# Four lanes in place of two in the last two node stages of a four-layer graph network

## The chip, the cores and the metric

The kernel runs on one core of one Trainium2 chip. The metric is the time on the device in microseconds, from one launch of the whole program. Three runs of the kernel before were timed.

## The reference

Four graph layers run one after the other on 6250 nodes of 128 features and 206250 directed edges. After each layer the input is added to its output and the sum is normalized over the features (mean 0, variance 1). Layer 0 sums edge features per target node and sends the sum and the node through a two-layer network. Layer 1 is edge attention with two norms and a feed-forward part. The two layers that matter here end in node work:

```
# layer 2: edges through a network, summed per target, then a network per node
agg  = segment_sum(relu(e_in @ We1 + be1) @ We2 + be2, dst)
x    = layernorm(x + (x + relu([x, agg] @ Wn1 + bn1) @ Wn2 + bn2))
# layer 3: sum over edges weighted by the degrees of both ends
deg  = segment_sum(1, row);  norm = deg[row]**-0.5 * deg[col]**-0.5
x    = layernorm(x + segment_sum(norm * x[col], row) @ W.T + b)
```

## The kernel before, in words

Node features stand transposed in SBUF: `x` and `acc` are [128 features, 6656 columns], the columns padded from 6250 nodes. They are cut into 26 tiles of T = 256 columns (TJ = 2 halves of 128). The program is a row of blocks, one after the other, each with a queue written out by hand for every engine: prepare, edge sums, layer0_nodes, layer1_edges, layer1_nodes, layer2_edges, **layer2_nodes** (line 1819), layer3_edges, **layer3_nodes** (line 2132). Only the two in bold are changed. Each starts when the block ahead of it has ended on all engines.

A node stage runs 13 steps (STEPS) of two tiles, the lanes (LANES = 2). In a step each engine goes through its phases in a fixed order, and in each phase over the lanes. An engine waits for a semaphore ahead of a piece of work, so lane 1 can fill the time in which lane 0 travels to another engine and back, but no engine starts the next step before its last phase of this one. The loops are hardware loops; offsets into `x`, `acc` and `counts` come from a register. `bank(l, b)` gives each lane four PSUM banks of its own, of which a tile of 256 fp32 columns fills half of one.

The phases of TensorE in layer2_nodes are, in order: **A**, L1834 (`We2` by `acc`) and L1836 (`be2` by the edge counts, which stand on 2 rows); **B**, L1839 and L1842 (the two halves of `Wn1`, the second after ScalarE has copied A's result, L1863); **C**, L1846 (`Wn2`, after ScalarE's ReLU, L1866); then the norm of `norm_pe`: **D**, L723 (subtract the mean, after VectorE's sum, L1900); **E**, L728 (variances, after ScalarE's squares, L741; results of one column); **F**, L734 (spread the inverse deviations, after ScalarE's root, L745, and VectorE's reciprocal, L750); and **G**, L1852 (two transposes, after VectorE's product L756). VectorE then scales the transposed rows (L1908), GpSimd splits them into three bf16 parts (four operations, L765 to L774), and SyncE stores them to DRAM (L1933), where layer3_edges reads them. Every matmul here is fp32 and appears as two passes.

In layer3_nodes TensorE's phases are: spreading four columns of degree factors over the partitions (L2143, four matmuls a tile), after VectorE's two small copies (L2167, L2168); L2149 (`W3`), after VectorE has done three dependent operations per tile (L2173, L2176, L2179); and D, E and F as above, after VectorE's L2184. VectorE's L756 ends a tile, and SyncE stores it to the output (L2197). GpSimd has no part in it.

What guards the reuse of a lane: TensorE's phase A waits until the rows of the same lane's tile of the step before have been scaled (`y_scaled`); VectorE's L1908 waits until GpSimd has split that tile (`split_step`); GpSimd waits for that tile's store (`y_stored`); VectorE's L756 in layer 3 waits for the output store (`out_stored`).

Of the kernel before, what the change touches and what calls it, by code (L numbers as in the profile page):

```python
# [5 lines left out]
P = 128  # L6
D = 128
# [7 lines left out]
T = 256  # L15
TJ = T // P
# [26 lines left out]
def gnn_program(nc, xT, edge_attr, src_index, src_id, dst_id, dst_rows, consts,  # L43
# [18 lines left out]
    with ctx:  # L62
# [647 lines left out]
        out_stored = [sem(f"out_stored{l}") for l in range(LANES)]  # L710

        def node_tiles(scope, layer):

            tiles = {name: [sb(f"{name}{layer}_{l}", [P, T], scope=scope) for l in range(LANES)]
                     for name in ("tmp", "res", "cen", "sqr", "y", "y2")}
            tiles["std"] = [sb(f"std{layer}_{l}", [P, TJ], scope=scope) for l in range(LANES)]
            tiles["inv"] = [sb(f"inv{layer}_{l}", [P, TJ], scope=scope) for l in range(LANES)]
            return tiles

        def norm_pe(pe, t, nth, ready, count_of):  # L720
            for l in range(LANES):
                pe.wait_ge(ready, count_of(l) + 1)
                nc.tensor.matmul(bank(l, 1)[:, 0:T], centre_m, t["res"][l][:, :], start=True, stop=True  # L723
                                 ).then_inc(centred_ps, 1)
            for l in range(LANES):
# [5 lines left out]
            for l in range(LANES):  # L731
# [6 lines left out]
        def norm_act(act, t, nth):  # L738
            for l in range(LANES):
# [3 lines left out]
            for l in range(LANES):  # L743
# [3 lines left out]
        def norm_dve(dve, t, nth, y_free=None):  # L747
            for l in range(LANES):
                dve.wait_ge(std_ready, nth + l + 1)
                dve.reciprocal(t["inv"][l][:, :], t["std"][l][:, :]).then_inc(inverse_ready, 1)  # L750
            for l in range(LANES):
# [1055 lines left out]
        y_stored = [sem(f"y_stored{l}") for l in range(LANES)]  # L1807
        nth2 = 4 * NTILES
        with ExitStack() as scope:
            t = node_tiles(scope, 2)  # L1810
            relu2_sb = [sb(f"relu2_{l}", [P, T], scope=scope) for l in range(LANES)]
            node_rows = [sb(f"y_f{l}", [P, TJ, D], scope=scope) for l in range(LANES)]
            y_parts = [sb(f"y_parts{l}", [P, TJ, 3, D], BF16, scope=scope) for l in range(LANES)]
            rest = [sb(f"y_rest{l}", [P, TJ, D], scope=scope) for l in range(LANES)]
# [4 lines left out]
            with nc.Block("layer2_nodes") as block:  # L1819
                @block.tensor  # L1820
                def _(pe):
# [6 lines left out]
                    with loop(pe, 0, STEPS) as n:  # L1828
                        def tile(l):
                            return n * LANES + l  # L1830

                        for l in range(LANES):
                            pe.wait_ge(y_scaled, tile(l) * TJ + TJ)
                            nc.tensor.matmul(bank(l, 0)[:, 0:T], we2_sb[:, :], acc[:, columns(tile(l))],  # L1834
                                             start=True, stop=False)
                            nc.tensor.matmul(bank(l, 0)[:, 0:T], be2_rows[:, :], counts[:, columns(tile(l))],  # L1836
                                             start=False, stop=True).then_inc(agg_ps2, 1)
                        for l in range(LANES):
                            nc.tensor.matmul(bank(l, 2)[:, 0:T], wn1_sb[:, 0, :], x[:, columns(tile(l))],  # L1839
                                             start=True, stop=False)  # L1840
                            pe.wait_ge(agg2, tile(l) + 1)
                            nc.tensor.matmul(bank(l, 2)[:, 0:T], wn1_sb[:, 1, :], t["tmp"][l][:, :],  # L1842
                                             start=False, stop=True).then_inc(hidden_ps2, 1)
                        for l in range(LANES):
                            pe.wait_ge(hidden2, tile(l) + 1)
                            nc.tensor.matmul(bank(l, 0)[:, 0:T], wn2_sb[:, :], relu2_sb[l][:, :],  # L1846
                                             start=True, stop=True).then_inc(mlp2, 1)
                        norm_pe(pe, t, nth2 + n * LANES, sum2, tile)
                        for l in range(LANES):
                            pe.wait_ge(normed, nth2 + tile(l) + 1)  # L1850
                            for j in range(TJ):
                                nc.tensor.transpose(bank(l, 2 * j)[:, 0:P], t["y"][l][:, j * P:(j + 1) * P],  # L1852
                                                    ident).then_inc(y_ps, 1)

                @block.scalar
                def _(act):
                    act.wait_ge(degree, 3)
                    act.activation(dis[:, :], deg_raw[:, :], ACT.Sqrt).then_inc(degree_sqrt, 1)
                    with loop(act, 0, STEPS) as n:
                        load_sqrt_table(act)  # L1860
                        for l in range(LANES):
                            act.wait_ge(agg_ps2, n * LANES + l + 1)
                            act.activation(t["tmp"][l][:, :], bank(l, 0)[:, 0:T], ACT.Copy).then_inc(agg2, 1)  # L1863
                        for l in range(LANES):
                            act.wait_ge(hidden_ps2, n * LANES + l + 1)
                            act.activation(relu2_sb[l][:, :], bank(l, 2)[:, 0:T], ACT.Relu,  # L1866
                                           bias=v("bn1")).then_inc(hidden2, 1)
                        norm_act(act, t, nth2 + n * LANES)
                        for l in range(LANES):
                            act.wait_ge(normed, nth2 + n * LANES + l + 1)  # L1870
                            act.activation(x[:, columns(n * LANES + l)], t["y"][l][:, :], ACT.Copy).then_inc(x_kept, 1)

                @block.vector
                def _(dve):
# [17 lines left out]
                    with loop(dve, 0, STEPS) as n:  # L1892
                        for l in range(LANES):
                            c = n * LANES + l
                            dve.tensor_scalar(t["y2"][l][:, :], x[:, columns(c)], 2.0, v("bn2"), ALU.mult,
                                              ALU.add).then_inc(twice2, 1)
                        for l in range(LANES):
                            dve.wait_ge(twice2, n * LANES + l + 1)
                            dve.wait_ge(mlp2, n * LANES + l + 1)
                            dve.tensor_tensor(t["res"][l][:, :], bank(l, 0)[:, 0:T], t["y2"][l][:, :],  # L1900
                                              ALU.add).then_inc(sum2, 1)
                        norm_dve(dve, t, nth2 + n * LANES)
# [364 lines left out]
```

## Time and profile before

| | us |
|---|---|
| median of 3 runs (lowest, highest) | 5868.11 (5867.2, 5871.65) |
| the profiled execution's own time | 5868.77 |
| its span, first to last instruction | 5866.9 |
| PE, matmuls: busy | 5316.1 (91%) |
| DVE busy | 4674.9 (80%) |
| ACT busy | 2572.2 (44%) |
| POOL busy | 2071.5 (35%) |
| mean granted TensorE clock | 0.965 of full speed |

The profile is of one execution. PE is TensorE's matmuls and PEld its weight loads, DVE is VectorE, ACT ScalarE, POOL GpSimd, SP SyncE. Times in the trace count from the span's start, and L1834 is line 1834 of the kernel before. In a view of busy time by stretch, PEclk is the clock that TensorE was granted, 1.00 for 2.4 GHz and 0.50 for 1.2 GHz. In the timeline, operations of one kind that follow each other are merged: "x8" means eight of them in that time, and a matmul's end is modelled.

### The profile page before, as it was taken

The numbers are of one execution on the slowest core, as the hardware profiler recorded it, in microseconds if no ns is written. First come the engines' busy times: TensorE is split into PE (matmuls) and PEld (weight loads), VectorE is DVE, ScalarE is ACT, GpSimd is POOL, SyncE is SP. The second block draws the span as 40 slices with busy tenths as digits, with TensorE's granted clock in tenths as the row PEclk, the third lists the DMA queues.
The fourth block names the chain that finished last, engine by engine and source line by source line (L and its number), as shares of the span: only waits on it lengthen the run. The fifth ranks groups of instructions, "written<-read, shape, count | busy, mean of one in ns | idle before, by whom it ended". The sixth has DMA issues, their size and how long they took to land. (4 is left out here: it accounts for less than half of the span.)

```text
span 5866.9 us, 170714 instructions
## 1 busy us (share of the span) xinstructions
PE 5316.1 (91%) x58518; PEld 4689.3 (80%) x58518; DVE 4674.9 (80%) x8022; ACT 2572.2 (44%) x5031; POOL 2071.5 (35%) x1980
## 2 busy tenths in 40 slices
PE   2999989799999999999997779999999997699987
PEld 2888877699999999999995569999999995466645
DVE  6999962588888888888884469999999993488874
ACT  0000024344444344444432347777777762366641
POOL 1444436333333333333332335555555551100000
PEclk9999999999999999999997989999999997899978
DMA  7444421222222222222220123333333330100000
GB/s 114 153 152 152 152 84 68 96 95 92 92 94 90 94 92 92 92 89 97 92 85 17 38 90 130 133 133 131 129 134 131 132 107 17 54 0 1 0 1 24
DMA packets 206213, 523.68 MB, mean 89 GB/s; under 512 B 33555, under 2 KB 85398, under 8 KB 199318
## 3 DMA queue, kind: packets, MB, share of 16 engines
q1 hardware_dynamic: 195936, 518.35, 26.1%
q10 hardware_dynamic: 10179, 4.02, 0.3%
q8 instruction: 62, 1.02, 0.1%
q14 instruction: 36, 0.29, 0.0%
HBM read 485.12 MB, written 37.19 MB: 89 GB/s over the span
## 5 line engine op out<-in xcount | busy, mean ns | idle before, releaser
L1276 PE MATMUL ps<-kv_table,stage 128*128 128x256 bf16 x7644 | 1252.8, 273 | 29.2 <-DVE stage L1132 27.5
L1556 POOL TENSOR_TENSOR parts<-rest 128x512 bf16<-128x512 f32 x624 | 699.4, 1130 | 622.5 <-DVE rest L1609 622.3
L1201 ACT ACTIVATE q_kept<-ps 128x512 f32<-128x512 f32 (+1 forms) x676 | 392.5, 581 | 1157.5 <-PE ps L1279 1157.5
L1746 PE MATMUL ps<-a_table,stage 128*128 128x128 bf16 x7644 | 843.6, 219 | 33.6 <-DVE stage L1585 33.6
L1749 PE MATMUL ps<-window,stage 128*128 128x128 bf16 x7800 | 862.8, 220 | 0.0
L1279 PE MATMUL ps<-window,stage 128*128 128x128 bf16 x7800 | 861.2, 220 | 0.0
L1248 POOL TENSOR_TENSOR message<-message 128x512 f32<-128x512 f32 (+1 forms) x468 | 482.0, 1030 | 986.7 <-ACT message L1210 986.6
L1276 PEld LDWEIGHTS ps<-kv_table,stage 128*128 128x128 bf16 x7644 | 667.6, 98 | 70.7 <-issue 28.1
L1279 PEld LDWEIGHTS ps<-window,stage 128*128 128x128 bf16 x7800 | 654.2, 98 | 59.5
L1140 DVE TENSOR_TENSOR product<-ps,q_kept 128x512 f32<-128x512 f32 (+1 forms) x676 | 451.2, 667 | 300.3 <-ACT message L1203 261.0
L1746 PEld LDWEIGHTS ps<-a_table,stage 128*128 128x128 bf16 x7644 | 534.5, 98 | 34.1 <-issue 34.0
L2075 PE MATMUL ps<-pairs,y_window 128*128 128x512 bf16 (+1 forms) x2028 | 532.2, 371 | 28.0 <-ACT pairs L2043 28.0
L1749 PEld LDWEIGHTS ps<-window,stage 128*128 128x128 bf16 x7800 | 545.7, 98 | 0.0
L1291 PE MATMUL ps<-message,slot_hot 128*128 128x136 f32 x3536 | 515.6, 288 | 32.6 <-POOL message L1248 32.5
L1665 ACT ACTIVATE parts<-ps 128x512 bf16<-128x512 f32 x624 | 370.4, 594 | 332.5 <-PE ps L1749 330.6
L2043 ACT ACTIVATE pairs<-ps 128x512 bf16<-128x512 f32 (+1 forms) x676 | 386.7, 572 | 259.4 <-PE ps L2067 210.4
L1760 PE MATMUL ps<-parts,slot_hot 128*128 128x258 bf16 x2496 | 491.1, 273 | 5.4 <-issue 3.5
L412 POOL TENSOR_TENSOR pay<-bucket_hot,vals 128x1550 bf16<-128x1550 bf16 x104 | 324.7, 3140 | 483.4 <-PE ps L393 370.8
L1291 PEld LDWEIGHTS ps<-message,slot_hot 128*128 128x128 f32 x3536 | 442.2, 190 | 50.6 <-POOL message L1248 32.2
L1762 PE MATMUL ps<-rest,slot_hot 128*128 128x128 bf16 x2600 | 476.8, 222 | 0.0
L1144 DVE TENSOR_REDUCE score<-product 128x32 f32<-128x512 f32 (+1 forms) x676 | 450.1, 666 | 23.2
L1152 DVE TENSOR_TENSOR slot_hot<-iota,slots 128x512 f32<-128x512 f32 (+1 forms) x676 | 454.0, 672 | 0.0
(350 smaller groups left out, 10473.0 us busy)
## 6 DMA issues: line engine op xcount, KB each, us to landing
stage<-lists SPq DMA_DIRECT2D x312, 768.0 KB, 4.1
edges<-in_edge_attr SPq DMA_DIRECT2D x52, 1984.0 KB, 7.7
stage<-lists SPq DMA_DIRECT2D x104, 896.0 KB, 5.4
window<-qkv_rows SPq DMA_DIRECT2D x52, 288.0 KB, 4.7
qkv_rows<-kv_table SPq DMA_DIRECT2D x26, 384.0 KB, 2.5
window<-ab_rows SPq DMA_DIRECT2D x52, 192.0 KB, 4.4
qkv_rows<-q_parts SPq DMA_DIRECT2D x26, 192.0 KB, 2.0
ab_rows<-a_table SPq DMA_DIRECT2D x26, 192.0 KB, 2.0
```

What stands on the lines that cost most here:

```text
L1140: dve.tensor_tensor(product[:, 0:nt, :], kv_ps[n % 2][:, 0:nt, 0:D], q_kept[n % 2][:, 0:nt, :], ALU.mult).then_inc(product1, 1)
L1152: dve.tensor_tensor(slot_hot[n % 2][:, 0:nt, :], over_chunks(iota1[:, :], nt), over_columns(slots[:, ds(g, 1), 0, 4 * b:4 * b + nt] .rearr ...
L1248: pool.tensor_tensor(values, values, message[n % 3][:, 0:nt, D:D + HEADS].unsqueeze(3) .broadcast_to([P, nt, HEADS, HEAD]), ALU.mult).then ...
L1276: nc.tensor.matmul(kv_ps[n % 2][:, i, :], from_src, kv_table[:, tile, q, :], start=(q == 0), stop=(q == 2))
L1279: last = nc.tensor.matmul(q_ps[n % 2][:, i, :], own, window[d][:, q * D:(q + 1) * D], start=(q == 0), stop=(q == 2))
L1291: last = nc.tensor.matmul(ps[:, 6 + d, 0:D + HEADS], slot_hot[n % 2][:, i, :], message[n % 3][:, i, :], start=(tile == 0), stop=(tile == S ...
L1556: pool.tensor_tensor(parts_of(n)[:, 0:nt, D:2 * D], rest[BUFFER[n]][:, 0:nt, :], middle[BUFFER[n]][:, 0:nt, :], ALU.subtract).then_inc(low ...
L1746: nc.tensor.matmul(to[:, i, :], from_src, a_table[:, tile, q, :], start=(q == 0), stop=False)
L1749: last = nc.tensor.matmul(to[:, i, :], own, window[d][:, (3 + q) * D:(4 + q) * D], start=False, stop=(q == 2))
L1760: nc.tensor.matmul(ps[:, 6 + d, 0:DIRECT], slot_hot[BUFFER[n]][:, :, i], parts_of(n)[:, i, :], start=(tile == 0), stop=False)
L1762: last = nc.tensor.matmul(ps[:, 6 + d, DIRECT:SUMS], slot_hot[BUFFER[n]][:, :, i], middle[BUFFER[n]][:, i, :], start=False, stop=(tile == ...
L2075: last = nc.tensor.matmul(ps[:, 4 + quad % 2, 0:nt * P], y_window[:, ds(i * 4 + d, 1), q * D:(q + 1) * D] .rearrange("p s f -> p (s f)"), ...
```

## The change

`WIDE` = 4 lanes are used in the two blocks. The 26 tiles go in six looped steps of four (`WIDE_STEPS`), and after the loop a seventh step of two (`REST_LANES`) is written out with constant offsets. A lane has two PSUM banks in place of four, and `half(l, b)` gives quarter b as half a bank, so that quarters 0 and 1 share one and quarters 2 and 3 the other. The tiles of SBUF that belong to a lane are doubled in number. The waits that guard reuse now look back four tiles. The operations and their number per tile, and their order within a lane, stay as they are; the order between lanes follows the loops. The other node stages keep two lanes and `bank`. The diff, cut:

```diff
+        WIDE = 4
+        WIDE_STEPS = NTILES // WIDE
+        REST_LANES = NTILES - WIDE * WIDE_STEPS
+        out_stored = [sem(f"out_stored{l}") for l in range(WIDE)]
+
+        def half(l, b):
+
+            return ps[:, 2 * l + b // 2, b % 2 * T:b % 2 * T + T]
+
+        def wide_steps(eng, step):
+
+            with loop(eng, 0, WIDE_STEPS) as n:
+                step(n, n * WIDE, WIDE)
+            if REST_LANES:
+                step(WIDE_STEPS, WIDE * WIDE_STEPS, REST_LANES)
...
-        def norm_pe(pe, t, nth, ready, count_of):
-            for l in range(LANES):
+        def norm_pe(pe, t, nth, ready, count_of, lanes=LANES, bank=bank):
+            for l in range(lanes):
...
@@ layer2_nodes, TensorE
-                    with loop(pe, 0, STEPS) as n:
+                    def step(n, first, lanes):
...
-                        for l in range(LANES):
+                        for l in range(lanes):
                             pe.wait_ge(y_scaled, tile(l) * TJ + TJ)
-                            nc.tensor.matmul(bank(l, 0)[:, 0:T], we2_sb[:, :], acc[:, columns(tile(l))],
+                            nc.tensor.matmul(half(l, 0), we2_sb[:, :], acc[:, columns(tile(l))],
                                              start=True, stop=False)
...
-                                nc.tensor.transpose(bank(l, 2 * j)[:, 0:P], t["y"][l][:, j * P:(j + 1) * P],
+                                nc.tensor.transpose(half(l, 2 * j)[:, 0:P], t["y"][l][:, j * P:(j + 1) * P],
                                                     ident).then_inc(y_ps, 1)
+
+                    wide_steps(pe, step)
...
@@ layer2_nodes, VectorE, GpSimd and SyncE
-                                dve.wait_ge(split_step, SPLITS2 + (n * LANES + l) * SPLITS + SPLITS - ROWS_AHEAD // 2)
+                                dve.wait_ge(split_step, SPLITS2 + (first + l) * SPLITS + SPLITS - SPLITS * WIDE)
...
-                            pool.wait_ge(y_scaled, c * TJ + TJ + LANES * TJ)
+                            pool.wait_ge(y_scaled, c * TJ + TJ + WIDE * TJ)
...
-                    sp.sem_inc(y_scaled, LANES * TJ)
-                    for l in range(LANES):
+                    sp.sem_inc(y_scaled, WIDE * TJ)
+                    for l in range(WIDE):
                         sp.sem_inc(y_stored[l], 16)
...
@@ layer3_nodes
-            t = node_tiles(scope, 3)
-            scales = [sb(f"scales{l}", [P, 2 * TJ], scope=scope) for l in range(LANES)]
+            t = node_tiles(scope, 3, WIDE)
+
+            def whole(l):
+
+                return ps[:, 2 * l, :]
+
+            scales = [sb(f"scales{l}", [P, 2 * TJ], scope=scope) for l in range(WIDE)]
...
-                                last = nc.tensor.matmul(bank(l, 0)[:, j * P:(j + 1) * P],
+                                last = nc.tensor.matmul(whole(l)[:, j * P:(j + 1) * P],
                                                         scales[l][:, j:j + 1].broadcast_to([P, P]), ident,
                                                         start=True, stop=True)
...
-                            pe.wait_ge(agg3, tile(l) * AGG + AGG + LANES * AGG)
-                            nc.tensor.matmul(bank(l, 2)[:, 0:T], w3t_sb[:, :], t["tmp"][l][:, :],
+                            pe.wait_ge(agg3, tile(l) * AGG + AGG + WIDE * AGG)
+                            nc.tensor.matmul(half(l, 2), w3t_sb[:, :], t["tmp"][l][:, :],
                                              start=True, stop=True).then_inc(lin3, 1)
...
-                        norm_dve(dve, t, nth3 + n * LANES, n)
+                        norm_dve(dve, t, nth3 + first, n, lanes, half)
+
+                    wide_steps(dve, step)
```

## Rows read from the trace of the kernel before

**Rows 1.** Busy time by stretch, both stages: window, length, busy us (instructions) by engine, PEclk, DMA, GB/s

```profile
4902.00:5051.60 149.60, 137.83 (x572) 89.03 (x572) 55.93 (x156) 57.49 (x168) 52.00 (x97) 0.93 0.09 32
...
5730.70:5863.60 132.90, 101.66 (x520) 81.92 (x520) 65.86 (x206) 24.92 (x90) 0.00 (x0) 0.88 0.07 24
```

**Rows 2.** Timeline, one step of layer2_nodes: start, us, engine, line, operation, [idle before <-releaser]

```profile
5006.42 0.69 PE L1834 MATMUL ps<-acc,we_sb 128*128 x2 [0.38 <-DVE y_f L1908]
...
5008.92 0.70 PE L1839 MATMUL ps<-x,wn_sb 128*128 x2
...
5009.89 0.59 PE L1839 MATMUL ps<-x,wn_sb 128*128 x2
...
5010.75 1.43 PE L1846 MATMUL ps<-relu,wn_sb 128*128 128x256 f32 x4
...
5012.01 1.45 PE L723 MATMUL ps<-res,cst 128*128 128x256 f32 x4
...
5012.67 0.38 ACT L741 ACTIVATE sqr<-ps 128x256 f32<-128x256 f32 x1 [1.24 <-PE ps L723]
...
5012.76 0.30 PEld L723 LDWEIGHTS ps<-res,cst 128*128 128x128 f32 x2 [0.54 <-DVE res L1900]
...
5014.56 1.05 PEld L734 LDWEIGHTS ps<-cst,inv 128*128 128x128 f32 x8
...
5015.38 0.95 DVE L756 TENSOR_TENSOR y<-cen,ps 128x256 f32<-128x256 f32 x2 [0.34 <-PE ps L734]
...
5015.86 0.97 PE L1852 MATMUL ps<-cst,y 128*128 128x128 f32 x4
...
5017.21 0.69 PE L1834 MATMUL ps<-acc,we_sb 128*128 x2 [0.39 <-DVE y_f L1908]
```

**Rows 3.** Timeline, first step of layer2_nodes

```profile
4902.05 1.22 PE L1834 MATMUL ps<-acc,we_sb 128*128 x2 [2.42 <-DVE self_dis L1891]
...
4906.64 1.22 PE L1839 MATMUL ps<-x,wn_sb 128*128 x2
...
4917.17 0.69 PE L1834 MATMUL ps<-acc,we_sb 128*128 x2 [0.38 <-DVE y_f L1908]
```

**Rows 4.** Timeline of PE, the step of layer2_nodes from 4960.33

```profile
4960.33 0.69 PE L1834 MATMUL ps<-acc,we_sb 128*128 x2 [0.38 <-DVE y_f L1908]
...
4962.83 0.96 PE L1839 MATMUL ps<-x,wn_sb 128*128 x2
...
4972.65 0.69 PE L1834 MATMUL ps<-acc,we_sb 128*128 x2 [0.39 <-DVE y_f L1908]
```

**Rows 5.** Busy time by stretch, three stretches of layer2_nodes

```profile
4902.00:4911.90 9.90, 9.85 (x20) 5.73 (x21) 0.72 (x3) 1.71 (x4) 0.00 (x0) 0.50 0.00 0
4963.20:4966.50 3.30, 3.30 (x9) 2.66 (x8) 0.00 (x0) 0.71 (x3) 2.15 (x5) 0.50 0.18 60
5015.90:5016.80 0.90, 0.81 (x4) 0.36 (x4) 0.79 (x3) 0.76 (x2) 0.00 (x0) 1.00 0.00 0
```

**Rows 6.** Timeline, last steps of layer3_nodes

```profile
5841.77 1.25 PE L734 MATMUL ps<-cst,inv 128*128 128x128 f32 x8
...
5844.08 3.52 PE L2143 MATMUL ps<-cst,scales 128*128 128x128 f32 x16 [1.06 <-DVE scales L2168]
...
5846.30 0.42 DVE L2173 TENSOR_TENSOR y<-x,ps 128x256 f32<-128x256 f32 x1 [2.02 <-PE ps L2143]
...
5854.61 2.05 PE L2143 MATMUL ps<-cst,scales 128*128 128x128 f32 x16 [1.06 <-DVE scales L2168]
...
5855.91 0.42 DVE L2173 TENSOR_TENSOR y<-x,ps 128x256 f32<-128x256 f32 x1 [1.10 <-PE ps L2143]
...
5857.25 0.42 DVE L2173 TENSOR_TENSOR y<-x,ps 128x256 f32<-128x256 f32 x1
...
5858.72 0.70 PE L2149 MATMUL ps<-tmp,w3t_sb 128*128 128x256 f32 x2 [0.64 <-DVE tmp L2179]
...
5859.46 0.48 DVE L2184 SCALAR_TENSOR_TENSOR res<-ps,vec,x 128x256 f32<-128x256 f32 x1 [0.40 <-PE ps L2149]
```

More of the change, by code:

```diff
@@ L730, in norm_pe @@
                 last.then_inc(variance_ps, 1)
-            for l in range(LANES):
+            for l in range(lanes):
                 pe.wait_ge(inverse_ready, nth + l + 1)
@@ L736, in norm_pe, with norm_act @@
                 last.then_inc(inverse_ps, 1)
-        def norm_act(act, t, nth):
-            for l in range(LANES):
+        def norm_act(act, t, nth, lanes=LANES, bank=bank):
+            for l in range(lanes):
                 act.wait_ge(centred_ps, nth + l + 1)
@@ L1835, in _ @@
                                              start=True, stop=False)
-                            nc.tensor.matmul(bank(l, 0)[:, 0:T], be2_rows[:, :], counts[:, columns(tile(l))],
+                            nc.tensor.matmul(half(l, 0), be2_rows[:, :], counts[:, columns(tile(l))],
                                              start=False, stop=True).then_inc(agg_ps2, 1)
-                        for l in range(LANES):
-                            nc.tensor.matmul(bank(l, 2)[:, 0:T], wn1_sb[:, 0, :], x[:, columns(tile(l))],
+                        for l in range(lanes):
+                            nc.tensor.matmul(half(l, 2), wn1_sb[:, 0, :], x[:, columns(tile(l))],
@@ L1840, in _ @@
                                              start=True, stop=False)
                             pe.wait_ge(agg2, tile(l) + 1)
-                            nc.tensor.matmul(bank(l, 2)[:, 0:T], wn1_sb[:, 1, :], t["tmp"][l][:, :],
+                            nc.tensor.matmul(half(l, 2), wn1_sb[:, 1, :], t["tmp"][l][:, :],
                                              start=False, stop=True).then_inc(hidden_ps2, 1)
-                        for l in range(LANES):
+                        for l in range(lanes):
@@ L1845, in _ @@
                             pe.wait_ge(hidden2, tile(l) + 1)
-                            nc.tensor.matmul(bank(l, 0)[:, 0:T], wn2_sb[:, :], relu2_sb[l][:, :],
+                            nc.tensor.matmul(half(l, 0), wn2_sb[:, :], relu2_sb[l][:, :],
                                              start=True, stop=True).then_inc(mlp2, 1)
-                        norm_pe(pe, t, nth2 + n * LANES, sum2, tile)
-                        for l in range(LANES):
+                        norm_pe(pe, t, nth2 + first, sum2, tile, lanes, half)
@@ L1891, in _, with step @@
                     dve.tensor_tensor(self_dis[:, :], self_dis[:, :], dis[:, :], ALU.mult).then_inc(degree, 1)
-                    with loop(dve, 0, STEPS) as n:
-                        for l in range(LANES):
-                            c = n * LANES + l
+                    def step(n, first, lanes):
+                        for l in range(lanes):
+                            c = first + l
                             dve.tensor_scalar(t["y2"][l][:, :], x[:, columns(c)], 2.0, v("bn2"), ALU.mult,
@@ L1896, in _ @@
                                               ALU.add).then_inc(twice2, 1)
[L1897 to L1900, printed above, removed]
+                        for l in range(lanes):
+                            dve.wait_ge(twice2, first + l + 1)
+                            dve.wait_ge(mlp2, first + l + 1)
+                            dve.tensor_tensor(t["res"][l][:, :], half(l, 0), t["y2"][l][:, :],
@@ L2134, in _, with step @@
                 def _(pe):
-                    with loop(pe, 0, STEPS) as n:
+                    def step(n, first, lanes):
                         def tile(l):
-                            return n * LANES + l
-                        for l in range(LANES):
+                            return first + l
+                        for l in range(lanes):
                             pe.wait_ge(scales3, tile(l) + 1)
@@ L2197, in _ @@
                             sp.dma_start(out[:, columns(c)], t["y"][l][:, :]).then_inc(out_stored[l], 16)
[L2198 to L2199 removed]
+                    wide_steps(sp, step)
+                    for l in range(WIDE):
+                        sp.wait_ge(out_stored[l], 16 * (WIDE_STEPS + (l < REST_LANES)) + 16)
                         sp.sem_inc(sp_waited, 1)
```

133 lines of the change are left out of this document (68 added, 65 removed).

## The prediction, made before the changed kernel ran

> **What bounds the kernel now.** TensorE is busy for 91% of the span, so at first sight more overlap has nothing to win. I read the busy time of the two changed stages alone [rows 1]: layer2_nodes takes 149.6 us, layer3_nodes 132.9, and nothing else of the kernel is touched. So at most 282.5 us are in play. The timeline of one step then shows what sets each stage's pace.
>
> In layer2_nodes a step takes 10.79 us at the full clock (its first and last row) [rows 2]. TensorE is in every link: it stops for ScalarE's and VectorE's answers (0.54 us ahead of the second L723, 0.39 ahead of the next step) and is otherwise at work or draining. VectorE is busy for 55.9 of 149.6 us, ScalarE for 57.5, GpSimd for 52.0 (2.0 us a tile) [rows 1]. In layer3_nodes TensorE is busy for 101.7 of 132.9 us and VectorE for 65.9; a step takes 10.53 us (5844.08 to 5854.61) [rows 6], in which the work travels in turn through L2143, three dependent VectorE operations, L2149, and the norm. There are 12 such intervals from 5730.7 to 5854.6, 10.33 us on average.
>
> The second thing to see is the clock. The granted mean is 0.93 in layer2_nodes and 0.88 in layer3_nodes [rows 1], that is 20.9 and 31.9 us at 1.2 GHz. In layer2_nodes it is low for the first 9.9 us, and three times for some 3.4 us (one of them in [rows 5]), each time where phase A ends: [rows 4] is such a step, of 12.32 us in place of 10.79. In layer3_nodes L2143 takes 3.52 us in a step that starts low and 2.05 in one that starts high [rows 6]; 31.9 us at some 3.4 each make nine of the 13 starts low.
>
> **The change, part by part.** No operation is added or removed, nor any DMA: 26 tiles with the same instructions, seven loop passes in place of 13. What goes is six of the hand-overs between steps and the waits inside a step that two lanes are too few to cover.
>
> *layer2_nodes, a step of four at full clock.* Per phase on TensorE, from [rows 2]: A took 2.50 us for two lanes, so 5.0 for four. B: 1.83 for two, 0.86 for each further lane (5009.89 to 5010.75), so 3.55. C and D are two passes of 256 columns a lane, as long as half of that 0.86, 0.43 each: 1.72 and 1.72, for the answer to lane 3's C is due some 0.7 + 0.42 us after it starts, and lanes 0 to 2 of D cover 1.29. E and F: 0.13 us for each of the weight loads (1.05 for eight), four a lane: 2.1 and 2.1. ScalarE needs at most 0.76 us a lane for squares and copies; it starts 0.66 after L723 and has lane 3's square at 0.66 + 3 x 0.76 + 0.38 = 3.3 us from D's start, and E wants it at 1.72 + 1.57 = 3.3: just covered. The first root comes after the last copy and is ready before F. G: lane 3's product starts 0.82 us after its F and F has 0.5 left, so 1.2 us for eight transposes with a short wait, and 0.4 to the next step. Sum: 5.0 + 3.55 + 1.72 + 1.72 + 2.1 + 2.1 + 1.2 + 0.4 = **17.8 us**, against 21.6 for two steps of two. The hidden work stays hidden: VectorE is busy for 2.2 us a tile, GpSimd for 2.0 and ScalarE for 2.2 (over 26 tiles) [rows 1], so 8 to 9 us of the 17.8 each; were TensorE not there, they would come next. VectorE's L1908 now runs twice as long at a step's end, but phase A's lane 0 wants only its first two operations, and so on lane by lane, 1.25 us apart. The stores on SyncE's queue keep their order and number; the last step still has two lanes, so the tail on GpSimd and SyncE is the old one.
>
> *The clock in it.* Phase A is where the clock fell, and it becomes twice as long in one piece. I expect a fall in each wide step instead of in one of four. A fall cost 12.32 - 10.79 = 1.5 us [rows 4, 2]; but if it comes early in a long A, the rest of A goes at 1.15 us an instruction ([rows 3]: 4.59 us for four) in place of 0.63 (2.50 for four) and more of B is caught at half speed. A long A of which 3 us are so stretched costs 2.5, and half of 3.5 us of B another 1.8: 4.3 as the upper end. I take 2.0, near the row. The first step starts low anyway: A costs 8 x 1.15 = 9.2 in place of 5.0, and 2 us more in B: 24.0, where the narrow one took 15.12 [rows 3]. The last step has two lanes: 10.79 and 0.6 to the end of VectorE's last rows, 11.4, and 0.3 for a fall in one of four, 11.7. Sum: 24.0 + 5 x 19.8 + 11.7 = 134.7, so **-14.9 us** of 149.6. Bounds: no fall at all after the first step, 24.0 + 5 x 17.8 + 11.4 = 124.4 (-25.2); falls that cost 4.3 us, 24.0 + 5 x 22.1 + 11.7 = 146.2 (-3.4).
>
> A sentence of the Trainium skill speaks against even this: "TensorE: Matmul & The Clock Gate", Part 4, says that transposes do not count as busy for the clock. The row here shows L1852 granted 1.00 (5015.90) [rows 5], so two lanes' worth does not bring it down; eight in a row, right ahead of A, are seen in no row. By that rule the clock would fall before A, and the stage would be the rival "long falls" below.
>
> *layer3_nodes, a step of four.* From [rows 6], full clock: L2143 takes 0.95 us a tile, 3.8 for four. VectorE starts its first product 1.30 after it and needs 1.34 a tile (5855.91 to 5857.25): last product of lane 3 done at 1.3 + 5.36 + 0.1 = 6.75. L2149 answers 0.7 later; four L2184 end at 8.3, the last L723 ends at 9.0, E at 11.1; lane 3's F starts at 12.7. From the second lane's F to the next L2143 the trace has 5844.08 - 5841.77 - 0.53 = 1.78, so the step is **14.5 us**. VectorE is the bound in its first half, TensorE in the second. A low start moves the first product from 1.30 to 2.22 and the last by about 1.25. I keep the share of low starts, two in three: 15.3 a step, 15.8 for the first, 9.6 for the last two lanes: 15.8 + 76.7 + 9.6 = 102.1, **-30.8 us** of 132.9. Bounds: none low, 15.8 + 72.5 + 9.0 = 97.3 (-35.6); the stretch in which TensorE waits for VectorE (3.8 to 7.5) lets the clock fall too, so that D and E go at half speed: six steps of 17.5 and 9.6, 114.6 (-18.3).
>
> *Leaving the loop.* The written-out last step comes after a loop's exit in the middle of the stage, which no row shows. The nearest is what a step boundary costs at all, 1.06 us of TensorE's waiting [rows 6]: between 0 and 2 us a stage. I take 0, as its code follows on directly.
>
> *Two quarters in one bank.* A matmul writes a quarter only after the other quarter of its bank has been read (C after A's copy, D after C's sum, F after E's root, G after D's copy), and engines at work on other lanes are in other banks. So it adds no wait.
>
> Sum: 5868.8 of the profiled execution less 14.9 and 30.8 is 5823.1. That execution lies 0.7 us above the median, which I leave: **5823 us**.
>
> **The rivals.**
>
> *The clock holds* (0.14). Denser work keeps it up. For it: C to G never brought it down. Against: A did, three times. Both stages at their upper bounds: 5868.8 - 25.2 - 35.6 = 5808.
>
> *Long falls* (0.20). The low stretch catches A's rest and B, and in layer 3 D and E. For it: in the first step the clock stayed low through A and most of B, 9.9 us, with TensorE busy 9.85 of them [rows 5], so being busy with A does not raise it. Then -3.4 and -18.3: 5847.
>
> *No overlap to win* (0.06). The phases of four lanes simply take twice those of two, as when an engine's own order, not waiting, sets the pace, and the waits of [rows 2] were filled by drains. Then 5868, within 1. Against it: layer 3's chain leaves TensorE idle for a quarter.
>
> *Slower: the clock stays low* (0.04). If wide steps never bring back 2.4 GHz after a fall, TensorE's own phases nearly double: A 9.2, B 6.9, C and D 3.4 each, E and F 4.2 each, G and the turn 2.5, 33.8 us for four tiles against 22.4 (twice the mean narrow step after the first, (149.6 - 15.1) / 12), +11.4 six times; layer 3 at about 24 against 20.7, +20: 5868.8 + 68 + 20 = 5957. In layer 2 it decides from about 9.2 us at 1.2 GHz in each wide step, where the 4.6 us won there are gone, and for the whole from some 12 us in the steps of both stages. Against it: B and C brought the clock back in every narrow step that lost it.
>
> **How the numbers follow.** The forecast has 0.56, and with its own bounds spans 5814 to 5838. With the clock holding (5808) and most of the long falls (5847) the range 5806 to 5849 holds 0.8. What this measurement can tell from no change is about 0.2%, 11.7 us. Faster by more: forecast, clock holding and nearly all of long falls, 0.88. Within: no overlap, 0.06. Slower: the low clock, and whatever a loop's exit or a wait that I overlooked adds, 0.06.
>
> **What would show it.** Wide steps in layer2_nodes of 18 to 21 us and in layer3_nodes of 14.5 to 16; no wait of TensorE for L1866, L1900 or L741 beyond the last lane's; granted means of 0.85 or so in layer 2, where most wide steps have one fall in A or B. A layer 2 step of over 22 us with a mean near 0.75 would be the long falls; steps of 21.6 at full clock would say that the overlap was never there. The stages ahead and layer3_edges between must stand as they are to 1 us; a loss there would be a cause I have not named.

## The result, and the profile after

The changed kernel takes **5804.39 us** (median of four, 5800.62 to 5809.88), against 5867.65 for the kernel before on the same chip: a ratio of 0.9894, 95% interval 0.988 to 0.9909, or 63 us less. The profiled execution took 5800.62 us, with a span of 5798.8. The forecast was 5823, with a range of 5806 to 5849: the direction was right, the gain was 63 us where 45 were predicted, and the time lies just outside the range.

The head of the page of the changed kernel:

```profile
span 5798.8 us, 170405 instructions
## 1 busy us (share of the span) xinstructions
PE 5270.3 (91%) x58518; PEld 4671.4 (81%) x58518; DVE 4666.6 (80%) x8022; ACT 2564.6 (44%) x5019; POOL 2070.9 (36%) x1980
```

TensorE's share is 91% as before, so the page alone still says nothing of where the time went. The busy time by stretch does; columns are those of [rows 1], and L2 and L3 stand for layer2_nodes and layer3_nodes from here on (L with three or four digits is a line). A stage's length runs from its first matmul to VectorE's last result; GpSimd's last splits of L2, some 5 us, come after it and count as time between the stages. First the two stages, then stretches inside them:

```profile
4895.50:5021.70 126.20, 123.61 (x572) 91.09 (x572) 51.10 (x156) 54.12 (x162) 51.33 (x97) 0.89 0.11 36
5703.60:5796.50 92.90, 77.75 (x520) 67.29 (x520) 62.74 (x206) 21.15 (x84) 0.00 (x0) 0.97 0.10 34
4923.20:4930.00 6.80, 6.80 (x16) 4.52 (x16) 0.00 (x0) 1.57 (x4) 5.25 (x11) 0.50 0.26 83
4943.70:4950.40 6.70, 6.70 (x16) 4.70 (x15) 0.00 (x0) 1.37 (x4) 5.23 (x11) 0.50 0.26 84
4958.40:4959.50 1.10, 1.10 (x10) 0.76 (x8) 1.07 (x4) 1.04 (x3) 0.00 (x0) 1.00 0.00 0
```

L2 takes 126.2 us in place of 149.6, L3 92.9 in place of 132.9 [rows 1]: -23.4 and -40.0. TensorE runs the same 572 and 520 instructions and VectorE the same 156 and 206; ScalarE runs six fewer in each stage, of an operation (L775) that comes once a step; the prediction had none removed. The mean granted clock went down in L2 (0.93 to 0.89) and up in L3 (0.88 to 0.97). Of the rest, the profiled execution reached L2 6.5 us earlier, in code that the change does not touch (the twelve kernels run here that are alike up to there reach it between 4895.1 and 4905.7, so this is scatter), the time between the stages, nearly all of it layer3_edges, grew by 2.9 us (679.0 to 681.9), and the end behind L3 is 1.1 us shorter.

TensorE's timeline through an L2 step that loses the clock (from 4939.50) and one that keeps it (from 4976.82). Lines have moved: L1848 and L1850 are phase A, L1853 and L1856 B, L1860 C, L737 D, L742 E, L748 F, L1866 G.

```profile
4939.50 0.69 PE L1848 MATMUL ps<-acc,we_sb 128*128 x2 [0.25 <-DVE y_f L1926]
...
4943.25 0.86 PE L1848 MATMUL ps<-acc,we_sb 128*128 x2
4944.04 1.22 PE L1850 MATMUL ps<-counts,be_rows 2*128 x2
4945.19 1.22 PE L1853 MATMUL ps<-x,wn_sb 128*128 x2
...
4959.80 0.69 PE L1848 MATMUL ps<-acc,we_sb 128*128 x2 [0.24 <-DVE y_f L1926]
...
4976.82 0.69 PE L1848 MATMUL ps<-acc,we_sb 128*128 x2 [0.24 <-DVE y_f L1926]
...
4981.83 0.70 PE L1853 MATMUL ps<-x,wn_sb 128*128 x2
...
4985.39 1.89 PE L1860 MATMUL ps<-relu,wn_sb 128*128 128x256 f32 x8
4987.12 1.89 PE L737 MATMUL ps<-res,cst 128*128 128x256 f32 x8
4988.84 1.84 PE L742 MATMUL ps<-mean_col,sqr 128*128 128x1 f32 x16
4990.55 2.03 PE L748 MATMUL ps<-cst,inv 128*128 128x128 f32 x16
4992.41 1.19 PE L1866 MATMUL ps<-cst,y 128*128 128x128 f32 x8
4993.84 0.69 PE L1848 MATMUL ps<-acc,we_sb 128*128 x2 [0.24 <-DVE y_f L1926]
```

From its start to the next is 17.02 us for the second (4976.82 to 4993.84) and 20.30 for the first (4939.50 to 4959.80). The one wait left inside is 0.24 us at the turn. The whole stage: 23.64 for the first step, 20.31 and 20.30 for two with a fall, 17.02, 17.02 and 16.9 for three without, and 10.96 for the last two lanes. A fall costs 3.3 us, and the clock is then at 1.2 GHz for some 6.8 us: the end of A and most of B. After the first step it falls nowhere else in this stage, and it is 1.00 while the eight transposes of G run (4958.40 above). The Trainium skill, "TensorE: Matmul & The Clock Gate", Part 4, says that transposes do not count as busy in the same way as other matmuls. The prediction read from it that the clock would fall before A. It did not: the two falls began some 4 us after A's start (4923.2 in the step from 4919.2, 4943.7 in the one from 4939.5). Whether 1.2 us of transposes have a part in a fall that comes so much later, these rows do not show.

L3's timeline, first step, then a warm one; L2172 spreads the scales, L2178 is the product with `W3`:

```profile
5703.62 6.03 PE L2172 MATMUL ps<-cst,scales 128*128 128x128 f32 x32 [4.94 <-DVE scales L2202]
...
5760.50 3.83 PE L2172 MATMUL ps<-cst,scales 128*128 128x128 f32 x32 [1.10 <-DVE scales L2202]
5764.17 1.14 PE L2178 MATMUL ps<-tmp,w3t_sb 128*128 128x256 f32 x4
5765.94 0.70 PE L2178 MATMUL ps<-tmp,w3t_sb 128*128 128x256 f32 x2 [0.63 <-DVE tmp L2213]
5767.27 0.70 PE L2178 MATMUL ps<-tmp,w3t_sb 128*128 128x256 f32 x2 [0.63 <-DVE tmp L2213]
5767.81 1.89 PE L737 MATMUL ps<-res,cst 128*128 128x256 f32 x8
5769.54 1.84 PE L742 MATMUL ps<-mean_col,sqr 128*128 128x1 f32 x16
5771.24 2.03 PE L748 MATMUL ps<-cst,inv 128*128 128x128 f32 x16
5774.36 3.83 PE L2172 MATMUL ps<-cst,scales 128*128 128x128 f32 x32 [1.09 <-DVE scales L2202]
```

A step takes 13.9 us (5760.50 to 5774.36), and only the first starts low (6.03 us for L2172, later 3.83). That is so in each of the eight traces here with four lanes in L3. The wait at the turn, 1.1 us, is as long as in the narrow kernel, but there are 6 such waits in place of 12. The waits by releaser, first of L2, then of L3, say it in total (us, times, longest):

```profile
PE ps L1848 <- DVE self_dis L1909: 2.4, 1, 2.4
PE ps L1848 <- DVE y_f L1926: 1.3, 5, 0.3
...
PE ps L2172 <- DVE scales L2202: 11.2, 7, 4.9
PE ps L2178 <- DVE tmp L2213: 8.1, 13, 0.6
```

In L3 TensorE's idle time fell from 31.2 us to 15.2 (stage less busy time, [rows 1]). In L2 it fell from 11.8 only to 2.6, which is less than the 23.4 won. The other part is "busy" time, 137.8 down to 123.6: the profile counts a matmul's latency to its end as busy, and with four lanes the next lane's work begins inside it. L723 took 1.45 us for 4 instructions [rows 2] and now 1.89 for 8. Time of this kind does not show as a wait.

### The profile page after: what moved, and what is told of

The parts are those of the page before. It is cut to its first block and busy times, and to the rows that moved or that the text cites. A ratio compares the mean times of both kernels' runs of the same rounds, so it can differ in the third digit from the quotient of the medians.

```text
span 5798.8 us, 170405 instructions
## 1 busy us (share of the span) xinstructions
PE 5270.3 (91%) x58518; PEld 4671.4 (81%) x58518; DVE 4666.6 (80%) x8022; ACT 2564.6 (44%) x5019; POOL 2070.9 (36%) x1980
## 3 DMA queue, kind: packets, MB, share of 16 engines
q8 instruction: 64, 1.05, 0.1%
```

## The experiments

### Each stage alone, packing alone, three lanes

In `l2_only` and `l3_only` one stage has four lanes, and the other runs the changed code with two. `two_packed` has two lanes in both: the changed code, with two quarters of a tile in one bank, and no added overlap. `three` has three lanes. The first block stands ahead of L3 in `l3_only`:

```
-        WIDE = 4
+        WIDE = 2          # l3_only, two_packed; three: 3
...
+        WIDE = 4          # ahead of layer3_nodes. l2_only, two_packed: 2; three: 3
+        WIDE_STEPS = NTILES // WIDE
+        REST_LANES = NTILES - WIDE * WIDE_STEPS
```

> Four lanes in layer2_nodes alone; layer3_nodes has two lanes in the packed banks. If each stage gains by its own overlap, layer2_nodes takes 120 to 130 us (126.2 in the changed kernel's trace, 149.6 before) and layer3_nodes 132 to 134, so the time is about 5844. If the gain is mostly one of layer 3's clock, the same, so this run alone does not tell them apart; if the two stages help each other it is over 5850.

> Four lanes in layer3_nodes alone; layer2_nodes has two lanes in the packed banks. Each stage by itself: layer2_nodes 147 to 152 us, layer3_nodes 92 to 94 with wide steps of 13.9 us that start at 2.4 GHz, so about 5828. If layer 3's clock held only by chance of phase in the one trace, some of its steps start low here and the stage takes 95 to 100.

> The changed code with two lanes in both stages: packed banks, the same helpers, 13 looped steps, no written-out rest. If lanes are the cause: 149 and 133 us, the time of before, 5867 within 4. If the packing or the way of writing the loops brings something: steps of layer 2 under 10.7 us, and a time under 5860.

> Three lanes in both stages, eight looped steps and a rest of two. If a step is TensorE's phases in a row and one hand-over: layer 2 steps of 13.1 to 13.3 us at full clock, layer 3 steps of 11.0, stages of 123 to 133 and 98 to 106, a time of 5811 to 5825. If four lanes bring nothing over three because two lanes of cover are enough, it equals the changed kernel, 5804. Clock theory for layer 3 (a low start comes from the share of the step in which TensorE waits): low starts in some of the eight steps, fewer than the nine of 13 with two lanes and more than none with four.

Measured against 5866.89 (13 runs) of the kernel before, run together with them; stage lengths from one trace each, good to 0.1 us:

| kernel | us | ratio (95%) | L2 | between | L3 |
|---|---|---|---|---|---|
| before | 5866.89 | 1 | 149.6 | 679.0 | 132.9 |
| two_packed | 5862.90 | 0.9996 (0.9987 to 1.0006) | 151.1 | 678.4 | 133.9 |
| l2_only | 5842.89 | 0.9953 (0.9936 to 0.9969) | 126.3 | 681.8 | 131.1 |
| l3_only | 5825.51 | 0.9928 (0.9911 to 0.9944) | 151.1 | 678.9 | 93.1 |
| three | 5817.82 | 0.9918 (0.9902 to 0.9935) | 135.4 | 678.5 | 101.9 |

Packing two quarters into a bank and cutting the loop's body out as a function are worth nothing that these runs can tell (the interval allows 0.1% either way): `two_packed` is the kernel before, with steps of 10.79 us at full clock as there. The two stages add up: 24.0 and 41.4 us alone, 65.4 together, 63.3 measured. Three lanes lie between: a warm L2 step takes 13.48 us for three tiles (4.5 a tile, after 5.4 with two and 4.25 with four), a warm L3 step 11.48 (3.8 a tile, against 3.5 with four). So it is overlap, it comes from the number of lanes, and by these rates it is nearly used up at four in L2. All four times are within 5 us of what was expected. One expectation on the clock is not: with three lanes fewer of L3's steps were to start low, but some; apart from the first, none did.

### Which part of L3's gain is the clock

In the narrow L3 most steps start low. `filled_narrow` is the kernel before with two matmuls, whose result nobody reads, put at the end of each L3 step, where TensorE waits 1.06 us [rows 6]:

```
                         norm_pe(pe, t, nth3 + n * LANES, sum3, tile)
+                        for _ in range(2):
+                            nc.tensor.matmul(bank(0, 2)[:, T:2 * T], w3t_sb[:, :], x[:, 0:T], start=True, stop=True)
```

> The kernel before with two more matmuls (w3t by x[:, 0:256], into a free half of a bank) at the end of each layer 3 step, where TensorE waits 1.06 us for VectorE. Their results are not used. Clock theory: that wait is what lets the clock fall in eight of the 12 later steps, so low starts vanish, steps take 9.5 us and the stage 122 to 125 in place of 132.9, the time about 5857. Rival: the two matmuls delay the step as much as they help (they end after the wait would), or falls come from the variances and spreads in D to F; then 131 us or more.

Its busy time over L3, and TensorE's timeline over one step:

```profile
5727.20:5851.50 124.30, 100.92 (x571) 77.87 (x572) 65.30 (x206) 24.91 (x90) 0.00 (x0) 0.98 0.07 25
```

```profile
5793.89 1.03 PE L2153 MATMUL ps<-x,w3t_sb 128*128 128x256 f32 x4
5795.12 2.05 PE L2143 MATMUL ps<-cst,scales 128*128 128x128 f32 x16 [0.20 <-DVE scales L2170]
...
5803.39 1.03 PE L2153 MATMUL ps<-x,w3t_sb 128*128 128x256 f32 x4
5804.62 2.05 PE L2143 MATMUL ps<-cst,scales 128*128 128x128 f32 x16 [0.20 <-DVE scales L2170]
```

L3 is 8.6 us shorter (132.9 to 124.3) with 52 more matmul passes in it (122 to 125 were expected); the granted mean is 0.98, and after the first every step takes 9.5 us. The kernel took 5857.12 against 5865.93, 0.999 (0.9981 to 0.9999). So the narrow kernel's low starts came from how little TensorE did around the turn of a step, and they were worth 8.6 us. The wide kernel loses them without any filling. Of its 40.0 us, then, about 8.6 are the clock and 31.4 the overlap. The division holds if the two do not act on each other, which was not tried. It also moves with the trace: in `l2_only`, whose L3 has two lanes too, six of the 12 later steps start low in place of eight, and in the four traces with two lanes and no filling (before, `before_pad`, `two_packed`, `l2_only`) the stage takes 131.1 to 135.0, so the clock's part is 7 to 11 us.

### What makes the clock fall in L2

The falls begin in phase A while TensorE is busy all the time. A alternates two full matmuls (`acc`, 128 rows) and two with an operand of 2 rows (`counts`). `no_counts` leaves `be2` times the counts out of layer2_nodes. `grouped` keeps it, but runs the four lanes' `We2` first and then the four lanes' `be2`:

```
                             nc.tensor.matmul(half(l, 0), we2_sb[:, :], acc[:, columns(tile(l))],
                                              start=True, stop=False)
+                        for l in range(lanes):
                             nc.tensor.matmul(half(l, 0), be2_rows[:, :], counts[:, columns(tile(l))],
```

> The changed kernel without L1850, so be2 times the edge counts is left out of the sum. Theory of the rows change: A takes 4 x 0.43 = 1.7 us, a wide step 13.7, and the clock does not fall after the first step, since the 2-row matmuls are what brings it down: stage about 90 us, time about 5768. If TensorE's waiting or the transposes ahead of A bring the clock down instead, falls of some 3.3 us remain in two or more of the steps.

> The changed kernel with phase A of layer2_nodes regrouped: L1848 for all four lanes, then L1850 for all four. Theory: what makes A slow (0.63 us an instruction where others take 0.43) is the change between operands of 128 rows and of 2 rows, once per instruction; now it comes twice a step, so A takes 3.9 in place of 5.0 us and a wide step 15.8 to 16.2 at full clock. Six steps: 6 to 7 us less than the changed kernel, 5797. Rival: the 0.33 us before each of them are the engine's work on register offsets; then A stays at 5.0 and the time at 5804. On the clock: if the mixture in A is what brings it down, there are no falls after the first step or fewer.

Busy time over L2, `no_counts` and then `grouped`, and `grouped` over one low stretch:

```profile
4905.70:5001.90 96.20, 93.53 (x520) 78.59 (x520) 51.06 (x156) 54.12 (x162) 50.32 (x94) 0.98 0.14 45
```

```profile
4898.80:5011.80 113.00, 110.40 (x572) 88.96 (x572) 51.00 (x155) 54.17 (x162) 51.32 (x96) 0.95 0.13 40
4953.30:4957.10 3.80, 3.80 (x11) 3.11 (x11) 0.00 (x0) 1.33 (x3) 3.05 (x6) 0.56 0.26 84
```

The low stretch at the start of L2's first step, in the changed kernel, `no_counts` and `grouped`:

```profile
4895.50:4909.50 14.00, 13.95 (x27) 7.86 (x28) 0.82 (x4) 2.48 (x6) 0.00 (x0) 0.50 0.00 0
4905.70:4910.30 4.60, 4.55 (x11) 3.66 (x12) 0.82 (x4) 1.53 (x4) 0.00 (x0) 0.50 0.00 0
4898.80:4902.50 3.70, 3.69 (x8) 2.52 (x8) 0.78 (x3) 0.00 (x0) 0.00 (x0) 0.50 0.00 0
```

Phase A of `grouped` in its timeline:

```profile
4966.93 2.41 PE L1848 MATMUL ps<-acc,we_sb 128*128 x8 [0.25 <-DVE y_f L1927]
4969.27 1.99 PE L1851 MATMUL ps<-counts,be_rows 2*128 x8
4971.19 0.70 PE L1854 MATMUL ps<-x,wn_sb 128*128 x2
```

Without the 2-row matmuls no step after the first has a fall in this trace (steps of 14.0 to 14.2 us); the mean is 0.98 and L2 takes 96.2 us, where about 90 were expected (A takes 2.25 us in place of the 1.7 assumed, because VectorE frees a lane only every 0.59 us). The removal of 52 of 572 instructions took off 30.0. Of these, 14.4 are the work itself in five steps (17.02 to 14.13), 6.6 the falls, 7.6 the first step (16.0 in place of 23.64) and 1.4 the last.

In `grouped` phase A takes 4.26 us (4966.93 to 4971.19) in place of 5.01 with the same instructions, so a change between an operand of 128 rows and one of 2 costs time: 0.75 us over the six changes less, some 0.12 each or more, for the grouped L1848 is held up in addition: its eight take 2.41 us where L737's eight take 1.89, because VectorE's L1927 frees the lanes one after another. The rival on record, the engine's work on register offsets, would have left A at 5.0. The first step of `grouped` takes 17.66, and it has two falls, as the changed kernel has; they come later, leave the clock low for some 3.4 us instead of 6.8 (0.56 on average over the 3.8 us of the row) and cost 1.6 (17.9 against 16.3). L2 is 13.2 us shorter than in the changed kernel: 6.0 in the first step, 3.4 in what the falls cost, 3.6 in the shorter A of the five steps after it. The whole kernel takes 5795.19 us in `grouped`, 0.9886 (0.987 to 0.9901), and 5787.01 in `no_counts`, 0.9865 (0.985 to 0.9881), against 5865.93 before. For `no_counts` about 5768 was expected. Those intervals overlap the changed kernel's: L2's gain reaches the end only in part, as layer3_edges takes 2.3 and 5.3 us longer here than in the changed kernel (below), and scatter ahead of L2 is of the same size.

For the clock, the evidence is of two strengths. That the alternation of 128 and 2 rows holds the clock down is borne out by several traces: in the five with four lanes and an alternating A the clock stays low for 13.1 to 14.7 us of the first step, and each of their 12 falls lasts 6.8; in `grouped` and `l1_wide_grouped` it is 3.7 and 2.9, and each of three falls lasts 3.4. The first step says more than the falls: with two lanes and an A of half the length falls last 3.4 us too, alternating as it is, but the first step's low stretch is 7.7 to 10.3 even there. That without the 2-row matmuls the clock does not fall at all rests on one trace of five steps, and `after_pad` below, which has them, shows no fall in five steps either. What the chip weighs in them is not shown.

### How much of the falls is chance

`after_again` is the changed kernel with an empty line at its end. `after_pad` has 24 waits of TensorE, long fulfilled, after L2, so that all later code of its queue is moved; `before_pad` has the same in the kernel before:

```
                     wide_steps(pe, step)
+                    for _ in range(24):
+                        pe.wait_ge(y_ps, 1)
```

> The changed kernel once more, unchanged, for its spread and for where the clock falls. Theory of carried phase: at full clock a wide step of layer 2 takes 17.0 us and then every later one does too, with a fall 20.3 and then the next has one too, so the trace shows a run of 20.3 and then a run of 17.0, with 0 to 5 of the five steps after the first at 20.3 (2 in the changed kernel's trace, 2 in that with layer 2 alone, 5 in that with layer 1 widened). The time lies between 5796 and 5812, median 5804. If falls are independent from step to step, long and short steps alternate.

> The changed kernel with 24 waits more on TensorE's queue after its last transpose of layer 2 (all satisfied at once, about 1 us while GpSimd still works). Theory of code position: the matmuls of layer3_edges from L2099's first to its last take 597 us in the kernels with two or three lanes and 599 to 605 in those with four, with TensorE idle 0.5 us in every third stretch of 50, because the instructions written out between its loops have moved; 24 more move them again, and the 599.7 changes by over 1 us either way. If it comes from what layer 2 leaves behind (stores, the clock), it stays at 599 to 600. The time 5804 within 5 in either case.

> The kernel before with the same 24 waits after layer 2's loop on TensorE's queue. Theory of code position: the matmuls of layer3_edges from L2075's first to its last, 596.9 us in the kernel before, change by over 1 us although layer 2 itself is untouched. If the 3 us that the four-lane kernels lose there come from layer 2's shorter run, they stay at 596 to 597.5. The stages: 149 to 151 and 132 to 134 us.

| kernel | us | steps of L2 after the first | L2 | falls |
|---|---|---|---|---|
| after | 5804.39 | 20.31, 20.30, 17.02, 17.02, 16.90 | 126.2 | 2 |
| l2_only | 5842.89 | 20.32, 20.37, 17.02, 17.03, 16.89 | 126.3 | 2 |
| after_again | 5801.59 | 20.32, 20.37, 20.31, 17.09, 20.17 | 132.7 | 4 |
| after_pad | 5806.21 | 17.03, 17.02, 17.03, 17.09, 16.88 | 120.0 | 0 |

The times are medians; steps, L2 and falls are those of the one profiled execution, which for `after_again` is its slowest, 5815.38. Up to L2's end these run the same instructions on every engine. `l1_wide` below, with the same L2 behind another layer 1, has four falls (20.27, 20.30, 20.30, 20.30, 16.89), not the five that the expectation gives it. So 0 to 4 falls come and go with the execution, worth 0 to 13 us. That is as large as the scatter between runs of one kernel (9.3 us for the changed one, 17.6 in `after_again`), but it does not explain all of it: of the 14.7 us between the spans of these two in the trace, 8.4 lie ahead of L2 and 6.5 in L2's falls. That the falls come in one unbroken run from the first step on, as the first two rows of the table suggest, is contradicted by `after_again`, where a step at full clock stands between two with falls. What decides it stays open.

The second question was the 2.8 us that layer3_edges lost; the prediction had said that a loss there of over 1 us would be a cause it had not named. From its first matmul of pairs to its last (5100.2 to 5697.1 before, 5070.6 to 5670.3 after) it takes 596.9 us in the kernel before and 599.7 in the changed one. It takes 596.3 in `two_packed` and `l3_only`, whose L2 has two lanes and no step written out behind the loop, 597.3 in `three`, which has one, 599.3 in `l2_only`, 599.1 in `after_again`, 602.0 in `grouped`, 602.8 in `after_pad` and 605.0 in `no_counts`; in `before_pad` 597.9 (5865.95 against 5863.09 for one run each). So the stretch varies by up to 8 us with its own instructions untouched, and padding added 3.1 to the changed kernel but only 1.0 to the old one. A position of the code that matters would fit the padding, but not `grouped`: its trace lists as many instructions on every queue of L2 as that of the changed kernel, so that nothing behind L2 has moved, and it still takes 2.3 us more, where two traces of the same code (the changed kernel and `after_again`) differ by 0.6. The cause is open.

### The same change one stage earlier, and both together

layer1_nodes has three norms a step and was still narrow. `l1_wide` gives it four lanes in the same way (its core; `nth1`, the buffers and the guard on `split_step` follow):

```
-                    with loop(pe, 0, STEPS) as n:
+                    def step(n, first, lanes):
...
-                        norm_pe(pe, t, nth1(n, 0), sum1a, tile)
+                        norm_pe(pe, t, nth1(first, lanes, 0), sum1a, tile, lanes, half)
...
+                    wide_steps(pe, step)
```

`l1_wide_grouped` is this with the regrouped phase A.

> The changed kernel with four lanes in layer1_nodes as well (packed banks, same helpers). A step of two takes 20.9 us there. TensorE needs about 6.2 us a tile and VectorE about the same, so a step of four takes 28 to 33 us in place of 41.9; the stage 190 to 215 in place of 272, the time 5725 to 5755. If SBUF or GpSimd (5.3 us a tile, 21 a step) bounds it, the step is not under 33.

> Four lanes in the node stages of layers 1, 2 and 3, with phase A regrouped: the two best variants together. The changed kernel's 5804 less 9 for the regrouping and 70 for layer 1: about 5725, the same stages as in the runs of each (layer 2 about 113 us, layer 3 92.9). If they interact, layer 2 or layer 1 differs from its own run by over 3 us.

Busy time over layer1_nodes, in the kernel before and in `l1_wide`:

```profile
3135.20:3425.10 289.90, 230.42 (x1040) 169.14 (x1040) 129.84 (x363) 105.33 (x310) 101.94 (x193) 0.90 0.10 33
```

```profile
3134.80:3347.70 212.90, 178.59 (x1040) 154.96 (x1040) 130.62 (x363) 91.36 (x297) 103.91 (x193) 0.95 0.14 45
```

77 us less for this stage, and within what was expected of it (190 to 215 us). `l1_wide` takes **5734.15 us**, 0.9773 (0.9758 to 0.9789); `l1_wide_grouped` **5712.27**, 0.9738 (0.9725 to 0.9752), against 5869.93 before. That is 158 us below the kernel before, and by the ratios some 91 below the changed one (0.9894 less 0.9738, of 5868). Here the regrouping shows in the whole kernel too: 0.0035, or 20 us, with intervals that do not overlap; about 5725 was expected. Part of the 20 us is the luck of the falls: L2 takes 132.2 us in the trace of `l1_wide`, which has four, and 111.8 in that of `l1_wide_grouped`, which has one.

## Why the prediction was right in its mechanism and short in its size

**Right.** Where the time lies (two stages, nothing else), that four lanes fill TensorE's waits and drains, that VectorE sets L3's first half, that the sum is over stages, that packing and leaving the loop cost nothing in the two stages (the step that leaves it takes 16.9 and 13.5 us, no longer than the others), that A is where L2's clock falls. The rival "no overlap" fell with `l2_only` and `l3_only`, "long falls" and "the clock stays low" with the steps above. "The clock holds" (0.14, 5808) came nearer to the measured time than the forecast did. In L3 it is what happened; in L2 it did not in the changed kernel's trace and did in `after_pad`'s, the same code with no fall.

**The terms that failed.** Two steps of the prediction failed: in L3 it kept the narrow step's share of low starts (4.2 us, measured 0), and in both stages it priced the weight loads of E and F at 0.13 us each (measured 0.107 and 0.116), which is most of the 7.5 us by which its wide steps were too long. A third term, L2's falls, was off in number and in size. The sum was 134.7 and 102.1 us, measured 126.2 and 92.9, so 17.7 us too much. Term by term:

| term | predicted | measured | off |
|---|---|---|---|
| L2, falls in five steps | 5 x 2.0 = 10.0 | 2 x 3.3 = 6.6 | 3.4 |
| L3, low starts after the first | 4.2 | 0 | 4.2 |
| L2, five warm steps | 5 x 17.8 = 89.0 | 85.0 | 4.0 |
| L3, five warm steps | 5 x 14.5 = 72.5 | 69.0 | 3.5 |
| first and last steps, four in all | 61.1 | 58.5 | 2.6 |

*The clock, 7.6 us.* For L3 I wrote "I keep the share of low starts, two in three". That share belonged to the narrow step: `filled_narrow` shows that it goes as soon as TensorE has more to do, and more to do is what the change brings. In the changed kernel no step after the first starts low, nor in `three` with its steps of 11.5 us. I treated the clock as a property of the stage and not of the step's filling. In L2 it was the reverse error in two halves that partly cancelled: a fall in each wide step where 2 of 5 came (0 to 4 in other traces), and 2.0 us for one, near the narrow row's 1.5, where 3.3 was right. My own upper end, 4.3, came from the mechanism that proved true: the fall catches the rest of a long A and most of B. How large this term's error came out is luck: I had 10.0 us, measured were 6.6 here, 13 with the four falls of `after_again` and 0 in `after_pad`.

*The warm steps, 7.5 us.* By phase, A took 5.01 (predicted 5.0), B 3.56 (3.55), C and D 1.73 and 1.72 (1.72 each). E took 1.71 and F 1.86 where I had 2.1 each, and G with the turn 1.43 in place of 1.6. The 0.13 us for a weight load came from a row of eight that took 1.05 [rows 2]. In eight instructions of two lanes the start of each lane is part of that time; sixteen in a row go at 0.107 and 0.116. I had removed this kind of wait from C and D but kept it in E and F. The same two phases make L3's step 13.9 in place of 14.5.

*The range.* Its lower end rested on "the clock holds", 124.4 + 97.3 = 221.7 us. Measured were 219.1 with two falls still in them. An end worked out with over-sized steps is no end: the range varied the clock and the falls but not the pace of a warm step, which I held to be known.

Between the two profiled executions lie 68.1 us of span, 63.4 of them in the two stages. The rest is 6.5 for the earlier start of L2 (scatter) and 1.1 behind L3, less the 2.9 that the time between the stages took back. That the medians differ by 63.3, so near to the stages' 63.4, is in part luck, for each kernel's stages are read from one execution.

## What to carry to other kernels

When lanes are added to a stage, price each phase by its rate over many instructions in a row, not by its time in the narrow step divided by the count: hand-overs and drains, which the profile books as busy, are what the lanes remove. Do not carry the narrow step's clock pattern over: work out again how TensorE is filled, and see whether the phase where it falls gets longer. And look at the neighbours: the same edit in layer1_nodes was worth more than in both stages here, and reordering small matmuls took 20 us more off that version, in part by fewer falls.

## What the runs showed of the hardware that was not expected

Matmuls with an operand of 2 rows, in turn with those of 128, go with a low granted clock although the engine shows as busy throughout. With the two kinds alternating, a fall left it at 1.2 GHz for 6.8 us, and the first step at 1.2 GHz for 13.1 to 14.7; with each kind in one run, 3.4 and 2.9 to 3.7. How many steps had a fall differed between executions of the same instructions, 0 to 4 of five. Switching between 128 and 2 rows costs some 0.12 us each time, or more. Eight fp32 transposes in a row, 1.2 us, ran at 1.00. And 1.1 us of waiting per step goes with low starts in the step of two lanes (10.5 us), not in that of four (13.9 us).
